# Attention on one Trainium2 core: output products placed ahead of the query or key piece in even steps

## The reference, cut to what matters

```python
xn = _layernorm(x)
x = x + _L1_attn_ref(xn, ...) + _L1_ffn_ref(xn, ...)     # 60 experts, top 4, and a shared one
# _L1_attn_ref: 16 heads, query/key width 64 + 64, value width 128
qs, ksem = xn @ wq_sem, xn @ wk_sem
qg, kg = _rope(xn @ wq_geo), _rope(xn @ wk_geo)
v = xn @ wv
scores = g * (qs . ksem) / 8 + (1 - g) * (qg . kg) / 8   # g: one gate per head
attn = softmax(causal(scores))
out = (attn @ v) @ wo
```

## Time and profile before

| | |
|---|---|
| median of 3 runs | 1824.44 us (1822.86 to 1836.78) |
| profiled execution | 1827.84 us, its span 1826.1 us |
| PE busy | 1696.7 us, 93% of the span, 9234 matmuls |
| PEld | 1360.4 us, 74% |
| DVE / ACT / POOL busy | 1194.3 (65%) / 1018.6 (56%) / 778.9 (43%) |
| mean granted TensorE clock | 0.976 of full speed |

### The profile page before, as it was taken

The page is one execution under the profiler, slowest core; times in us unless marked ns, Lnnn a source line. Parts: engine busy times, 40 slices in busy tenths (PEclk is TensorE's granted clock), DMA queues, the critical chain, the costliest instruction groups (busy, mean ns, idle before and its releaser), DMA issues. The chain is left out here.

```text
span 1826.1 us, 33417 instructions
## 1 busy us (share of the span) xinstructions
PE 1696.7 (93%) x9234; PEld 1360.4 (74%) x9234; DVE 1194.3 (65%) x2422; ACT 1018.6 (56%) x2287; POOL 778.9 (43%) x789
## 2 busy tenths in 40 slices
PE   6399999489999999999999999999998999999997
PEld 2256556378888888888888888888885777666775
DVE  4799973597887766766767676667662344333476
ACT  4599943267665656665666566666652444434322
POOL 1489861453234544434443444344431342211463
PEclk9699999799999999999999999999999999999999
DMA  4653238500000100000000000001006999999433
GB/s 148 262 221 110 97 116 273 180 12 1 15 9 7 41 13 21 21 6 26 14 11 20 20 20 20 6 26 47 18 30 218 322 325 313 313 302 304 138 95 91
DMA packets 100395, 193.29 MB, mean 106 GB/s; under 512 B 15460, under 2 KB 59748, under 8 KB 97748
## 3 DMA queue, kind: packets, MB, share of 16 engines
q1 hardware_dynamic: 58836, 108.76, 19.1%
q0 software_dynamic: 17152, 47.67, 8.1%
q10 hardware_dynamic: 24336, 35.98, 5.9%
HBM read 140.84 MB, written 51.51 MB: 105 GB/s over the span
## 5 line engine op out<-in xcount | busy, mean ns | idle before, releaser
L1435 POOL TENSOR_TENSOR sw<-sw,rope_t 64x512 f32<-64x512 f32 x128 | 166.1, 1297 | 520.7 <-ACT sw L1048 495.1
L1077 ACT ACTIVATE pb<-ps,negmax 128x128 f32<-128x128 f32 (+7 forms) x256 | 190.8, 745 | 151.2 <-DVE negmax L1288 148.1
L963 PEld LDWEIGHTS ps<-pt,v 128*128 128x128 f32 x1280 | 242.1, 190 | 42.1 <-DVE xr L1316 4.0
L963 PE MATMUL ps<-pt,v 128*128 128x256 f32 (+1 forms) x1280 | 270.7, 358 | 2.8 <-DVE xr L1316 2.6
L561 POOL DMA_DIRECT2D w2r<-in_w x148 | 77.2, 522 | 320.1 <-PE ps L610 278.4
L644 DVE SCALAR_TENSOR_TENSOR ga<-th,ps 128x176 f32<-128x176 f32 x148 | 49.9, 337 | 230.0 <-ACT th L625 230.0
L1288 DVE TENSOR_REDUCE negmax<-ps 128x1 f32<-128x128 f32 (+7 forms) x256 | 193.9, 758 | 8.8
L1064 ACT COPY pt<-ps 128x512 f32<-128x512 f32 (+3 forms) x384 | 171.5, 484 | 38.7 <-PE ps L953 35.6
L1438 POOL TENSOR_TENSOR t<-t,sw 64x512 f32<-64x512 f32 x128 | 167.8, 1311 | 19.2 <-POOL sw L1435 12.8
L593 PE MATMUL ps<-w13r,xt 128*128 128x352 f32 x496 | 169.4, 464 | 0.0
L953 PE MATMUL ps<-ident,pb 128*128 128x128 f32 x1152 | 167.5, 272 | 0.0
(11 more groups left out here) (245 smaller groups left out, 4004.6 us busy)
## 6 DMA issues: line engine op xcount, KB each, us to landing
w13r<-in_w SPq DMA_DIRECT2D x124, 352.0 KB, 5.5
w2r<-in_w POOLq DMA_DIRECT2D x148, 176.0 KB, 5.8
result<-yy ACTq DMA_DIRECT2D x148, 128.0 KB, 4.9
crow<-c_rows SPq DMA_DIRECT2D x32, 512.0 KB, 3.5
t<-sorted SPq DMA_DIRECT2D x124, 128.0 KB, 5.1
sorted<-zeros ACTq DMA_DIRECT2D x15, 1024.0 KB, 16.9
hc<-in_w SPq DMA_DIRECT2D x24, 352.0 KB, 5.1
wraw<-in_wqk SPq DMA_DIRECT2D x16, 256.0 KB
```

What stands on the lines that cost most here:

```text
L963: last = pe.matmul(ps[:, 6, c0:2 * P], v[:, j, hd], pt[g % 2][:, j, c0:2 * P], start=j == 0, stop=j == 2 * g + 1)
L1077: act.activation(pb[:, qt % 2, 0:cols], ps[:, bank:bank + 2, :].rearrange("p a n -> p (a n)")[:, 0:cols], ACT.Exp, bias=negmax[:, par, qn: ...
L1435: g.tensor_tensor(sw[64:128, p % 2, :], sw[64:128, p % 2, :], rope_t[64:128, 1, (p // 2) * 512:(p // 2 + 1) * 512], ALU.mult).then_inc(s_t ...
```

## The change

It changes the order of calls in even steps on three engines; the instructions stay the same but for waits.

- TensorE: `output` first, then `piece`. In sweeps with hh = 0 the output gets a wait of its own for the value pieces g that it reads (s_e7); the wait of the first turn's c = 3 for the routing's reads of bank 7 (s_rank) moves with the piece.
- ACT: `swap` becomes the last of an even step. At qt 2 and 4 the order is `rounded`, `take_output`, `exp_tile`, `swap`; at qt 0 and 6 `rounded`, `exp_tile`, `take_output`, `swap`.
- DVE: `output` (otl) ahead of `turned`.

```diff
@@ att_pe, body
-                        if qt in (2, 4, 6):
-                            pe.wait_ge(s_rank, qt // 2)
                     if qt % 2 == 0:
                         p, g = qt // 2, qt // 2 - 1
-                        if not last:
-                            if p == 0 and next_b == 0:
-                                pe.wait_ge(s_ws, 2 * hp + c // 3 * 2 + (1 - hh) + 1)
-                            piece(p, next_b, 1 - hh, piece_fill(pair, hh, p))
                         if g >= 0:
+                            if hh == 0:
+                                pe.wait_ge(s_e7, value_fill(pair, g))
                             output(it, g, hh)
                         elif not first(it):
                             if hh == 1:
                                 pe.wait_ge(s_e7, value_fill(pair, 3))
                             output(it - 1, 3, 1 - hh)
+                        if first_heads(hp) and c == 3 and p > 0:
+                            pe.wait_ge(s_rank, p)
+                        if not last:
+                            if p == 0 and next_b == 0:
+                                pe.wait_ge(s_ws, 2 * hp + c // 3 * 2 + (1 - hh) + 1)
+                            piece(p, next_b, 1 - hh, piece_fill(pair, hh, p))
@@ att_act, body
-                        if qt == 6 and not last:
-                            exp_tile(it, 8, hh)
+                        if qt in (2, 4):
+                            take_output(qt)
+                        if qt < 6 or not last:
+                            exp_tile(it, qt + 2, hh)
+                        if qt in (0, 6):
+                            take_output(qt)
                         if not last:
                             swap(act, n0 + p, p, piece_fill(pair, hh, p))
-                        if qt == 2:
-                            take_output(qt)
-                        if qt < 6:
-                            exp_tile(it, qt + 2, hh)
-                        if qt != 2:
-                            take_output(qt)
@@ att_dve, body
-                        if not last:
-                            turned(n0 + p, p)
                         if qt > 0:
                             output(it, qt // 2 - 1)
                         elif not first(it):
                             output(it - 1, 3)
+                        if not last:
+                            turned(n0 + p, p)
```

## The result

The changed kernel took 1911.2 us (median of 6 runs, 1902.7 to 1912.6) against 1827.7 for the kernel before: 1.0444 times as long, 95% interval 1.041 to 1.048. The forecast was 1889 within 1852 to 1922, slower. The profiled execution was the fastest of the six, 1902.7 us outside and 1901.0 inside the span, 74.9 more than before; where the median lies 8.5 us above it, no trace shows.

A forecast was written before the change was run, and what follows sets the result against it. TensorE was taken to bound the attention stage. Waits 48, splits 9 and routing 7 sum to +64 us: 1892 from the profiled 1827.8, forecast as 1889 because that run lay 3.4 above the median; range 1852 to 1922.

The forecast's parts named there:

- The ceiling of the gain and the waits that go: TensorE waits 2.3 us per pair, the most reordering can gain; three projection waits on otl go, about 1.9 per pair.
- The covers that go: TensorE work no longer hides DVE's chain from `turned` to `add_out`: per pair, outputs wait 4.07 us, value pieces 0.93.
- The pair: Two sweeps, hh = 0 and 1: new waits 5.4 us against 2.3, 3.1 more; +48 us over 15.5 pairs.
- The splits: DVE's new-weight splits at odd qt delay the swap: 1.0 us at c = 3, 0.3 at c = 2; 9 us altogether.
- The later sweeps: Sweeps behind the first eight: 11.5 pairs x 3.1 + 5 x 1.3 = 42 us more by the prediction's terms.
- The first eight sweeps: Start of the attention stage: 4 x 3.1 + 2 x 1.3 + 7 = 22 us more by the prediction's terms.
- the routing arithmetic: DVE, first six sweeps: some 13 split-sized pieces at odd qt cost 7 us, between 0 and 22.
- a clock still at 1.00: Sign in the changed profile that the prediction is right: the clock stays at 1.00.
- The covers do not hold: Rival that they hold: DVE's `add_out` precedes TensorE's next output, only the gain is left, 30 us, 1795; 7%.
- nothing cancels: Rival that gain and loss cancel: four output waits of 4.07 us shrink to 1.0, 1810 to 1842 us; 5%.
- The rotation: Rival: POOL's two products behind the swap make ACT's rounding wait, the next output 1 us late per sweep, about 1920; 8%.
- The bank rule: PSUM banks 6 and 7: by rotation alone only bank 7's 0.93 us is added, gain 1.9 outweighs it, about 15 us faster.

The follow-up runs named there:

- experiment one: The changed kernel with DVE's `turned` one step later, behind `add_out`, in sweeps with hh = 1 (except an early one): 1883.6 us, 1.0289 of the kernel before.
- six: The kernel before with the change at qt 6 alone, on all three engines: 1.0062 of the kernel before.
- experiment four: The changed kernel with the query-key split of c = 3 moved on DVE from qt 1 to qt 5: 1.0368 of the kernel before.
- experiment ten: The kernel before with the full change only from the third turn on, the first eight sweeps in the old order: 1.0257 of the kernel before.
- experiment eight: The changed kernel measured again without any edit: 1908.3 us, 1.0428 of the kernel before.
- experiment two: The kernel before with only TensorE's part of the change, ACT and DVE in the old order: 2026 us, 1.1055 of the kernel before.

## Why the prediction was right, step by step

- **The ceiling of the gain and the waits that go.** Right. The three projection waits went, 1.7 us per pair where 1.9 was taken, and the change could not have won more than they held.
- **The covers that go.** Right in the main. Predicted waits per pair 1.18, 0.58, 0.81, 1.50 on `add_out` and 0.62, 0, 0.31 on `turned`; measured as gaps 1.18, 0.45, 0.85, 1.16 and 0.70, 0, 0.20. The predicted ones hold the slower first matmul too, so they are better held against whole steps, from one transposes' start to the next one's: at hh = 1 the steps of qt 2, 4, 6 and the next qt 0 grew by 1.18, 0.53, 0.91 and 1.29 us in the mean, 3.9 against 4.07. The mechanism, `turned` in front of `add_out`, is shown by experiment one at qt 2 and for half of the wait at qt 0. At qt 4 it is argued: the order on DVE is the same, but that experiment's step is no shorter. At qt 6 it was wrong, as experiments one and six show, and the size was right by luck.
- **The pair.** Predicted +3.1, measured +3.44 (65.11 against 61.67). The difference is made of small terms of either sign: the first value piece waits longer (0.70 and a slower first matmul against 0.62), the projection at qt 7 of hh = 1 gives 0.2 instead of 0.32, and qt 0 costs less. The piece's slower start is not among them: behind an output it begins so much sooner that output and piece together take 2.1 us at qt 2, as before, where nothing waits.
- **The splits.** Predicted 1.0 per turn at c = 3 and 0.3 at c = 2, 9 us; at c = 3 the trace shows 1.28 more than at c = 1 (31.34 against 30.06 for the sweep), at c = 2 0.2 more than at c = 0, and experiment four takes 7.5 out by moving the first. Right, and the path was the one named, with the transposes as a second place of it. In the first turn it cost nothing.
- **The later sweeps.** By the prediction's terms 11.5 pairs x 3.1 + 5 x 1.3 = 42; measured 46.6, and 46.3 in experiment ten.
- **The first eight sweeps.** Here the sum was too small: 4 x 3.1 + 2 x 1.3 + 7 = 22, measured 30.6. If the eight lose by their place in the turn what the later ones do (1.7, 1.7, 2.0 and 3.0 us for c = 0 to 3), 17 us are accounted for and 14 are left, where the prediction had 7 for the routing arithmetic. Slower matmuls at the lower clock (last section) hold some 6.5 of these 14; the sum had no such term, and "a clock still at 1.00" is the one sign among those it named that did not come. The rest, some 7, is waits. TensorE's longest are there, up to 2.65 us at c = 3, qt 4, where DVE's `route1_base` and the reading of the ranks stand ahead of `add_out`, but so are waits for the values in the first sweep. No experiment separates these, and a slower TensorE may also have shortened some waits, so that the 7 that is left meets the 7 predicted is no evidence for the term.
- **The rest.** 48 + 9 + 7 = 64 was predicted, 77 is in the trace's stage and 84 between the medians. The 7 between the last two are within the scatter of the runs (1902.7 to 1912.6), and their place is not shown.
- **The rivals.** The covers do not hold and nothing cancels. The rotation did not become the wait: ACT waited 9.0 us for POOL's t in the whole stage of the changed kernel (2.4 before). It did so only where `turned` was made later still, in experiment one.
- **The bank rule.** By the Trainium skill (Perfetto Trace Analysis, Matmuls) independent matmul groups should rotate through PSUM banks; the trace agrees on bank 7, where value pieces now wait for `turned` to empty it. That is 0.9 of 4.9 us of gaps per pair (3.64 for `add_out`, 0.90 for `turned`, 0.38 for the values at qt 0). The prediction's orders 7-6-6-7 and 6-7-6-7 are those of hh = 0. At hh = 1, without value pieces, 7-6-6 became 6-7-6: bank 6 is used twice running either way, but before it was the projection that followed the output and waited for otr and otl, and now it is the next output that follows the projection and waits for `add_out`, which stands behind the maximum in DVE's queue. The 0.85 at qt 6 is of this kind, with no part of `turned` in it.

## What to carry to other kernels

When a call is moved to free one consumer, list what the moved block stood in front of: here it was the cover of another engine's queue, and DVE, waiting for ACT's swap copies and then at work on `turned`, held back work that was ready for 0.6 us of that wait. An in-order engine turns a wait for one bank into a wait for every bank whose work stands behind it. The same swap can win at one step (qt 2: 7.7 us less over the later 23 sweeps) and lose at another (qt 6: 12.6 us more), so price it step by step, and do not split a change over several engines into parts that were meant together.

## What the runs showed of the hardware that I had not expected

In the first eight sweeps of the changed kernel the granted clock fell. Three stretches of that trace: the one before the output at qt 6 of the first sweep, the output itself, and the piece behind it.

```profile
412.40:416.24 3.84, 2.02 (x20) 1.88 (x18) 3.81 (x8) 1.40 (x3) 2.07 (x1) 1.00 0.00 0
416.24:420.33 4.09, 4.09 (x13) 3.32 (x13) 2.12 (x11) 1.63 (x5) 0.00 (x0) 0.58 0.00 0
420.33:423.00 2.67, 2.67 (x20) 2.36 (x19) 0.42 (x1) 1.36 (x3) 0.00 (x0) 1.00 0.00 0
```
```profile
416.24 4.33 PE L963 MATMUL ps<-pt,v 128*128 128x256 f32 x12 [1.82 <-DVE v L1304]
```

TensorE had waited 1.99 us and been busy for 2.02 of 3.84; then twelve matmuls took 4.09 us where they take 2.40 in later sweeps, mostly at the lower of the two levels, 1.2 instead of 2.4 GHz: 1.7 us lost on top of the wait. The same happened behind a wait of 2.8 us in the fourth sweep (3.01 for the output at qt 4 instead of 1.54) and behind two of 2.8 and 2.5 us in the sixth (2.30 for the piece at qt 2 instead of 1.48, 3.98 for the output at qt 6). With the matmuls right behind them that is some 6.5 us in this kernel, so a chain of waits has a second price once single waits grow.

It is not a fixed price. The waits of up to 1.2 us in the later sweeps did not bring it: the clock is 1.00 there. In the fourth sweep a wait of 2.5 us, in front of the routing's counts, was not followed by a fall in this run, but was in experiment eight. And in experiment two the projection waits 2.0 us at qt 1 of every later sweep, and the clock fell nine times in these 23 sweeps (0.98 over the stretch). What decides between them was not tested.
